# Second attention of a four-block kernel: ScalarE takes three steps of the memory part, the next input rows are turned behind the first score half, and the value products go to the rows' PSUM bank

## What is computed

```python
# second attention (16 heads of 16)
x = x + tanh(g_xattn[1]) * (softmax(layernorm(x) @ Wq.T @ k.T / 4 + bias) @ v) @ Wo.T      # k, v from the context
# then x + tanh(g_ffn[1]) * memory(layernorm(x)); its first step, for each sequence, on x = layernorm(x):
q = slot_query                                                                     # 16 slots
scores = (q @ d_Wq + d_bq) @ (x @ d_Wk + d_bk).T / 4
o = q + (softmax(scores) @ (x @ d_Wv + d_bv)) @ d_Wo + d_bo
```

## Time and profile before

| | us |
|---|---|
| median of 3 runs | 1344.31 |
| lowest and highest run | 1343.42, 1347.88 |
| the profiled execution's own time | 1347.85 |
| its span | 1346.1 |
| second attention (first mixing on VectorE to the last memory output) | 791.36 to 1156.4 |

### The profile page before, as it was taken

The page is one execution under the profiler, slowest core; times in us unless marked ns, Lnnn a source line. Parts: engine busy times, 40 slices in busy tenths (PEclk is TensorE's granted clock), DMA queues, the critical chain, the costliest instruction groups (busy, mean ns, idle before and its releaser), DMA issues.

```text
span 1346.1 us, 38344 instructions
## 1 busy us (share of the span) xinstructions
PE 1280.9 (95%) x14758; PEld 1143.9 (85%) x14758; DVE 927.0 (69%) x2426; ACT 805.5 (60%) x1794; POOL 747.9 (56%) x836
## 2 busy tenths in 40 slices
PE   7999999997999999999999988999999998899898
PEld 6888888886899999999999977899999997555476
DVE  3899999997576566555555027999999997221386
ACT  3676776663666777777676435666666665332453
POOL 1377777765478777777876034566666643100231
PEclk8999999998999999999999989999999999999999
DMA  5665554543667676777766811631111110599811
GB/s 173 214 223 192 189 168 165 190 166 108 231 214 217 223 223 220 226 232 228 218 220 224 327 44 29 236 116 49 49 49 56 56 32 29 215 430 429 322 64 64
DMA packets 103892, 237.52 MB, mean 176 GB/s; under 512 B 8992, under 2 KB 86176, under 8 KB 91296
## 3 DMA queue, kind: packets, MB, share of 16 engines
q1 hardware_dynamic: 97568, 218.29, 47.1%
q0 software_dynamic: 6144, 16.79, 3.9%
HBM read 174.22 MB, written 60.82 MB: 175 GB/s over the span
## 4 chain that ended last, share of the span: by engine, by line
PE 86%; DVE 5%; DMA 3%; ACT 2%; issue 2%; SPq 0%; POOL 0%; DVEq 0%; ACTq 0%; PEldq 0%; POOLq 0%
PE ps L1640 13%; PE psT L1625 6%; PE ps L648 6%; PE psS L625 5%; PE ps L802 5%; PE ps L852 5%; PE psT L634 4%; PE ps L661 4%; PE psS L1625 3%; PE ps L1625 3%; PE ps L785 2%; PE ps L815 2%; PE ps L742 2%; PE psT L640 2%; PE ps L1878 2%
## 5 line engine op out<-in xcount | busy, mean ns | idle before, releaser
L1593 POOL TENSOR_TENSOR wb_lo<-arena,wb_hi 128x2048 fp32r<-128x2048 f32 x64 | 298.0, 4657 | 96.7 <-ACT wb_hi L1713 96.7
L1640 PE MATMUL ps<-wb_hi,hT_hi 128*128 128x256 f32 x528 | 152.0, 288 | 2.5 <-DVE hT_lo L1766 2.5
L634 PE MATMUL psT<-arena 32*128 32x128 f32 x2048 | 151.2, 286 | 0.4 <-ACT arena L955 0.4
L1640 PE MATMUL ps<-wb_lo,hT_hi 128*128 128x256 f32 x528 | 149.3, 283 | 0.0
L1640 PE MATMUL ps<-wb_hi,hT_lo 128*128 128x256 f32 x528 | 148.4, 281 | 0.0
L625 PE MATMUL psS<-arena 32*128 32x256 f32 x1024 | 142.8, 397 | 1.2 <-ACT arena L955 0.5
L1713 ACT CAST wb_hi<-arena 128x1024 fp32r<-128x1024 f32 x128 | 130.6, 1045 | 11.3 <-DMA arena<-w_dram 10.7
L634 PEld LDWEIGHTS psT<-arena 32*128 32x128 f32 x2048 | 126.5, 189 | 1.1 <-issue 0.6
L1236 POOL TENSOR_TENSOR arena<-arena,eps_sb 128x1 f32<-128x1 f32 x96 | 23.8, 248 | 164.7 <-DVE arena L1113 114.2
L1778 DVE TENSOR_TENSOR arena<-ps,arena 128x512 f32<-128x512 f32 (+1 forms) x39 | 25.4, 650 | 117.4 <-PE ps L1640 77.0
L625 PEld LDWEIGHTS psS<-arena 32*128 32x128 f32 x1024 | 95.2, 191 | 9.9 <-issue 6.7
(11 more groups left out here) (400 smaller groups left out, 3920.5 us busy)
## 6 DMA issues: line engine op xcount, KB each, us to landing
arena<-wset_dram SPq DMA_DIRECT2D x24, 2048.0 KB, 14.5
xs_rows<-arena SPq DMA_DIRECT2D x33, 1024.0 KB, 5.0
arena<-w_dram SPq DMA_DIRECT2D x32, 1028.0 KB, 6.0
arena<-w_dram SPq DMA_DIRECT2D x32, 1024.0 KB, 5.9
arena<-w_dram SPq DMA_DIRECT2D x7, 2052.0 KB, 13.5
w_sb<-xs_rows SPq DMA_DIRECT2D x33, 256.0 KB, 2.7
xs_rows<-arena SPq DMA_DIRECT2D x33, 256.0 KB, 5.6
arena<-ctxT_dram SPq DMA_DIRECT2D x63, 128.0 KB, 2.3
```

What stands on the lines that cost most here:

```text
L634: nc.tensor.matmul(psT[:, b, j * P:(j + 1) * P], kbd[p, (k - 1) % 3, c, par, :], qT[p, (k - 1) % 3, c, :], start=j == 0, stop=False, skip_ ...
L1593: nc.gpsimd.tensor_tensor(wb_lo[:, u % 2, part], wb_raw[:, u % 2, part], wb_hi[:, u % 2, part], ALU.subtract).then_inc(w_g.sem, 1)
L1640: last = nc.tensor.matmul(ps[5][:, t * D:(t + 1) * D], hp[:, f, t * P:(t + 1) * P], wp[:, f, :], start=f == 0 and t == 0 and n == 0, stop= ...
```

## The change

- **ScalarE takes three steps of the memory part.** The copy of the memory values to dVb and the product pn = exp * 1/z move from VectorE to ScalarE (one copy, and two activations with a scale, placed between the copy of ps[4] and the first exponential). The third, the negation of the maxima, is gone: the memory scores are made with the opposite sign, VectorE takes their minimum, and ScalarE's exponential has scale -1 with that minimum as bias.
- **The bias row of the memory values** (dbv) is no longer added to each item. Since the probabilities of a row sum to one, dbv @ d_Wo is added once to the output bias row dbo: two matmuls on ps[4] ahead of step -2 and one addition on VectorE.
- **The next input rows** (input_turned) stand right behind the first score half, and ScalarE copies them to xT right behind the first exponential.
- **The value products** go to the second half of ps[5] instead of ps[6]; TensorE waits ahead of them until the copy to xT is done, and ScalarE copies the keys out as soon as they are there, without waiting for the values.

```diff
@@ tensor, ahead of the steps
+                    for c in range(C):
+                        last = nc.tensor.matmul(ps[4][:, 0:D], col["dbv"][:, c:c + 1].to_broadcast([P, P]), w["do"][:, c, :],
+                                                start=c == 0, stop=c == C - 1)
+                    last.then_inc(setup_p, 1)
                 for k in steps:
                     if not A and k == 0:
                         pe.wait_ge(stash_a, STASH + LATE)
+                        pe.wait_ge(setup_v, 8)
...
                     scores(k, 0)
-                    if A and valid(k + 1):
+                    if valid(k + 1):
                         input_turned(k + 1)
...
                         keys(k + 1, 6)
-                        values(k + 1, 6)
+                        if not A:
+                            pe.wait_ge(pre_a.sem, pre_a.at(k + 1, "xT"))
+                        values(k + 1, 6 if A else 5)
...
-                    if not A and valid(k + 1):
-                        input_turned(k + 1)
...
-                        if A and k + 1 >= early:
-                            pe.wait_ge(kv_a.sem, kv_a.at(k + 1, "V"))
+                        if k + 1 >= early:
+                            pe.wait_ge(kv_a.sem, kv_a.at(k + 1, "V" if A else "K"))
@@ scalar, behind the copy of ps[4]
+                    if not A and valid(k - 5):
+                        act.wait_ge(x1_p.sem, x1_p.at(k - 5, "V"))
+                        before(act, x2_v.sem, x2_v.at(k - 6, "mask"))
+                        nc.scalar.copy(dVb[:, (k - 5) % 2, :], ps[5][:, D:2 * D]).then_inc(x1_a.sem, 1)
+                        act.wait_ge(x2_v.sem, x2_v.at(k - 5, "rz"))
+                        before(act, x2_p.sem, x2_p.at(k - 6, "pT"))
+                        for c in range(C):
+                            last = nc.scalar.activation(pn[:, c, :], sc[:, c, :], ACT.Identity, bias=0.0, scale=srz[:, c:c + 1])
+                        last.then_inc(x2_a.sem, 1)
...
-                    if A and valid(k + 1):
+                    if valid(k + 1):
                         act.wait_ge(pre_p.sem, pre_p.at(k + 1, "xT"))
-                        before(act, pre_p.sem, pre_p.at(k, "x"))
+                        before(act, pre_p.sem, pre_p.at(k, "x" if A else "Q"))
                         nc.scalar.copy(xT.rearrange("p c t -> p (c t)"), ps[5][:, 0:D]).then_inc(pre_a.sem, 1)
@@ vector
                     dve.wait_ge(a0_last["res"].sem, a0_last["res"].at(B - 1, "res"))
+                    dve.wait_ge(setup_p, 2)
+                    nc.vector.tensor_tensor(row["dbo"], ps[4][:, 0:D], row["dbo"], ALU.add).then_inc(setup_v, 1)
...
-                        nc.vector.tensor_tensor(pn, sc, srz[:, :, None].to_broadcast([P, C, P]), ALU.mult)\
-                            .then_inc(x2_v.sem, 1)
...
-                        nc.vector.tensor_scalar(snx, smx, -1.0, None, ALU.mult).then_inc(x1_v.sem, 1)
...
-                        nc.vector.tensor_tensor(dVb[:, rt_i % 2, :], ps[5][:, D:2 * D], row["dbv"], ALU.add)\
-                            .then_inc(x1_v.sem, 1)
```

More of the change, by code:

```diff
@@ L976, in scalar @@
                         nc.scalar.copy(x_all[:, k - 4], ps[4][:, 0:D]).then_inc(x1_a.sem, 1)
-                    if not A and valid(k + 1):
-                        act.wait_ge(pre_p.sem, pre_p.at(k + 1, "xT"))
-                        before(act, pre_p.sem, pre_p.at(k, "Q"))
-                        nc.scalar.copy(xT.rearrange("p c t -> p (c t)"), ps[5][:, 0:D]).then_inc(pre_a.sem, 1)
                     if A and k == -1:
@@ L1209, in vector @@
                                                 ALU.mult).then_inc(x2_v.sem, 1)
-                    if not A and valid(rt_i):
-                        dve.wait_ge(x1_p.sem, x1_p.at(rt_i, "V"))
-                        before(dve, x2_p.sem, x2_p.at(rt_i - 1, "av"))
-                        nc.vector.tensor_tensor(dVb[:, rt_i % 2, :], ps[5][:, D:2 * D], row["dbv"], ALU.add)\
-                            .then_inc(x1_v.sem, 1)
                     if not A and valid(sl_i):
```

47 lines of the change are left out of this document (22 added, 25 removed).

## The result

The changed kernel is slower. Ten runs of each gave a median of 1354.63 us (1349.23 to 1364.78) against 1348.82 us (1343.42 to 1351.28) for the kernel before; the ratio is 1.0069 with a 95% interval of 1.0043 to 1.0096. The prediction said slower as the likeliest, at 1349.3 us with a range up to 1354.0; the median lies 0.6 us outside it. It had added its 5.0 us to the 1344.31 of three runs of the kernel before, and the ten runs of that kernel have a median 4.5 us higher. Against them the change cost 5.8 us by the medians and 5.8 to 12.9 by the interval. Two later series of the changed kernel gave 1.0091 and 1.0110.

What follows compares the result with a forecast made beforehand. TensorE's own work was taken to bound the full steps, so relieving VectorE gains nothing. Start 2.8 plus the value products' wait 2.2 gave 5.0 us, added to the median for 1349.3 us; range 1344.8 to 1354.0.

Steps and rivals of the forecast that it cites:

- What bounds the kernel: Second attention: TensorE's list sets the 22 full steps; work taken off VectorE gives nothing; stashed steps stay at 10.05 us.
- VectorE is the bound after all: Rival: hidden waits in TensorE's list let VectorE's relief save up to 23 us, giving 1321; chance 0.10.
- Start, +2.8: Start of the second attention: the bias addition waits for TensorE and holds up VectorE's first mixing, +2.8 us.
- Clock, 0 with bounds of 1.4: Lower-clock stretch near the start: taken to move with the work, 0 us, bounds -1.4 to +1.4.
- The wait ahead of the value products, +2.2: Full steps: TensorE waits for ScalarE's copy to xT, 22 items x 0.10 = 2.2 us, bounds 0 and 7.7.
- Other waits, "covered by 0.3": Full steps: input_turned's wait for ScalarE's dVb copy is covered by 0.3 us, so it adds nothing.
- ScalarE late: Rival, full steps: scaled activations delay the first exponential 0.3 us, TensorE waits 0.35 for xT; 10.5 us, 1354.8; chance 0.15.
- Last items, 0 with bounds of 0.7: Tail: VectorE's 0.7 us relief set against pn standing ahead of ScalarE's x_all copy; 0, bounds -0.7 to +0.7.

Runs made afterwards that it cites:

- e7_all: Changed kernel with the bias addition behind the first normalisation, value products in ps[6], ScalarE's x_all copy first from the second tail step; 1346.82 us, 1.0007.
- e8_early_turn: Changed kernel with the bias addition behind the first normalisation, value products in ps[6], probabilities and value copy back on VectorE; 1345.90 us, 1.0002.
- b1: Kernel before with one added wait: VectorE's first mixing waits for the last product of TensorE's preamble; 1353.78 us, 1.0031.
- e2_bank6: Changed kernel with the value products back in ps[6] and no wait for the xT copy ahead of them; 1357.42 us, 1.0074.
- e3: Changed kernel with the bias addition behind the first normalisation and the value products back in ps[6]; 1352.30 us, 1.0040.
- e3_again: The e3 kernel unchanged, run again in a later series against the kernel before; 1351.04 us, 1.0027.

## Why the prediction was wrong

*The number*: the sum was 5.0 us and the runs gave 5.8 by the medians, but the sum was laid on 1344.31, the median of three runs, where ten gave 1348.82. Laid on that, it would have been 1353.8. So most of the 5.3 us between 1349.3 and 1354.63 come from the base, and 0.8 from the sum. The sum is near the medians partly by luck, since a term that was set to 0 below cost time and one that was counted came out smaller. Its range, too, does not follow from its terms at the lower end (1344.3 + 2.8 - 0.7 - 1.4 = 1345.0, not 1344.8).

*What bounds the kernel*: right. TensorE's list sets the full step, and VectorE's 28 us of relief gave nothing: 22 full steps take 234.7 us in e7_all with ScalarE's steps and 234.7 in e8_early_turn without them. The stashed steps of the first profile kept their 10.05. The rival "VectorE is the bound after all" is out. The Trainium skill (Perfetto Trace Analysis, Optimizing Scalar/DVE Operations) says that moving work to ScalarE may make sense where VectorE is saturated. At 93% beside a TensorE at 100% of the window it gained nothing here: 1.0002 for e8_early_turn, 1.0007 for e7_all.

*Start, +2.8*: right, measured +2.94. (TensorE's idle time is 3.62 and not the 4.4 forecast, since the two new matmuls fill 0.87 of it.) *Clock, 0 with bounds of 1.4*: mis-sized. The stretch at 1.2 GHz begins 13.4 us behind the last matmul of the layer ahead, and began 13.0 behind it before; it did not move with the work, and the first turned rows and queries now fall into it. (It is not fixed either: in the versions with the addition moved and ScalarE's steps in place it began 16.2 to 22.4 behind.) B grew by 1.3 in the first pair of profiles, and by 1.1 over the means of three and four (9.48 against 8.43). Start and clock together are 4 us; b1, which lacks the matmuls and the addition (1.2), shows 2.6.

*The wait ahead of the value products, +2.2*: mechanism right, size 1.3 on the chip of the first profiles (C: 235.8 against 234.5). The restart of 0.05 was right; the two activations cost 0.59, as taken, but the exponential was released on time. By the Trainium skill (PSUM — Partial Sum Buffer, section on PSUM bank collisions) one guards by bank. The runs show what the guard costs here, 0.05 a step in the first profile and 2.0 us in 22 steps on the chip of e2_bank6, and not what would happen without it.

*Other waits, "covered by 0.3"*: this failed in three of the six series. The cover was counted on one execution. Where the copy of the maxima comes later, it is gone, and the full steps cost 4.3 (239.2 against 234.9) instead of 1.3. That is the mechanism of the rival *ScalarE late* (1354.8, chance 0.15), reached by another way than its price for an activation.

*Last items, 0 with bounds of 0.7*: this is the step of the mechanism that failed. The text named the order (the probabilities ahead of the copy to x_all, behind mask and sum) and then set it off against VectorE's 0.7. Measured: 2.6 us on average of all versions, 1.6 for the changed kernel's own profiles against those of before, 3.9 in the first pair. The wait itself is small, 1.97 instead of 1.19 at the first scores, and the next wait, 0.51 instead of 1.92, gives it back. What the bounds left out is the clock: at equal 1.2 GHz the tails differ by 0.7, and the rest is that all eight profiles with the new order have 6.8 us or more of it, and three of the eight with the old one. That the longer wait brings it on fits these counts; it was not shown, since an item's waits together are shorter (2.48 instead of 3.11).

By the profiles' means: start 2.9 + clock 1.1 + full steps 1.3 + tail 2.6 = 7.9, less 1.5 behind the second attention, where the profiles of before have 3.4 us at 1.2 GHz and the changed kernel's have none, leaves 6.4 us; 9.4 on the chips with late copies. The runs gave 5.8 by the medians of the first series (9.3 by its ratio) and 14.4 and 14.5 by those of the two series on the other chips, where the intervals of the ratios reach down to 6.6 and 9.1. The 5 us between account and medians on those chips stay open, and so does whether the 1.5 us belong to the kernel: e8 has that stretch in one profile and not in the other, and of the versions of e3 only e3_again has it.

## What to carry to other kernels

An engine works its list in order, so moving an operation to an idle engine moves its waits too. Look at what stands behind it in every stage, the first and last steps above all, and put it behind whatever the bounding engine waits for. Idle time that covers a wait is to be read on more than one execution and chip before it is spent: 0.74 us of it looked free, and in three of six series about 0.3 of it was in use. A small sum done once does not belong ahead of a loop if it waits for an engine that the loop's first step doesn't need: that wait alone cost 3 to 4 us.

## What the hardware showed that was not expected

TensorE's clock. A wait of TensorE that became 0.8 us longer (1.97 instead of 1.19), or a new one of 1.30, was followed by 6.8 to 13.7 us at 1.2 GHz in all ten profiles that have one. In three of the ten others there was 6.8, in two 3.4, so such a wait is not needed for it. 6.8 us at 1.2 GHz cost the kernel before 39.1 - 37.05 = 2.1 us.

The copy of the maxima behind TensorE's transposition: in three series 0.25 to 0.30 us in all 32 items; in three others the same for items 0 to 4 and 28 to 31, and 0.46 to 0.75 for items 5 to 27, in both kernels. The rows do not show what holds it there, and no run was made to find out. Within a series all profiles are of one kind; each later series had one chip and one stretch of time, so that the chip makes the difference is likely and not shown.
